# A two-layer AdaLN transformer kernel: the stage between its two attentions, rewritten

## The reference, cut to what matters

```
y = attn @ Wproj
y = jnp.transpose(y, (0, 2, 1)).reshape(Bx, Sx, Hx)
return y @ Wproj
```

## Time and profile before

| | us |
|---|---|
| median of 3 runs (lowest, highest) | 2282.1 (2281.39, 2282.92) |
| profiled execution, its own time | 2283.89 |
| profiled execution, span of the trace | 2282.1 |
| `layer0_attention` | 0 to 1798.9 of the span |
| `layer0_out` | 1798.95 to 1947.8 |
| the two functions of layer 1 | 1948.1 to 2282.1 |

### The profile page before, as it was taken

The page is one execution under the profiler, slowest core; times in us unless marked ns, Lnnn a source line. Parts: engine busy times, 40 slices in busy tenths (PEclk is TensorE's granted clock), DMA queues, the critical chain, the costliest instruction groups (busy, mean ns, idle before and its releaser), DMA issues. The chain is left out here.

```text
span 2282.1 us, 45663 instructions
## 1 busy us (share of the span) xinstructions
PE 2114.3 (93%) x16684; PEld 927.0 (41%) x16684; DVE 1758.6 (77%) x4030; ACT 1551.3 (68%) x3249; POOL 654.6 (29%) x1219
## 2 busy tenths in 40 slices
PE   6799999999999999999999999999999698989983
PEld 5143333333333333333333333333332287567731
DVE  3888888888888888888888888888885277244477
ACT  2078787877878787878787787878787445146633
POOL 2214142332313232414233231313211044000077
PEclk8599999999999999999999999999999799999955
DMA  5230312222121303031222212130200300000001
GB/s 150 41 63 11 67 25 52 38 39 50 27 50 32 65 12 71 10 67 24 54 38 40 50 27 50 32 64 8 45 2 2 103 0 0 1 1 2 1 28 46
DMA packets 129528, 84.74 MB, mean 37 GB/s; under 512 B 90273, under 2 KB 119073, under 8 KB 129313
## 3 DMA queue, kind: packets, MB, share of 16 engines
q1 hardware_dynamic: 129312, 81.91, 18.2%
HBM read 26.81 MB, written 16.78 MB: 19 GB/s over the span
## 5 line engine op out<-in xcount | busy, mean ns | idle before, releaser
L755 ACT ACTIVATE probs<-b_bank 128x512 f32<-128x512 f32 (+1 forms) x2304 | 1171.8, 578 | 347.2 <-PE b_bank L915 336.1
L632 DVE TENSOR_REDUCE m_part<-a_bank 128x1 f32<-128x512 f32 (+3 forms) x2048 | 1190.5, 634 | 153.1 <-PE a_bank L885 111.0
L915 PE MATMUL b_bank<-q_pack,k_pack 34*128 34x512 bf16 (+7 forms) x5120 | 920.8, 348 | 4.4 <-DMA q_pack<-m_rows 2.9
L885 PE MATMUL a_bank<-k_pack,q_pack 64*128 64x512 bf16 (+3 forms) x2560 | 811.1, 357 | 54.3 <-DVE m_part L632 30.7
L957 PE MATMUL acc<-probs,v_tile 128*32 128x512 f32 (+3 forms) x5120 | 586.7, 539 | 3.1 <-POOL probs L498 0.8
L915 PEld LDWEIGHTS b_bank<-q_pack,k_pack 34*128 34x128 bf16 (+1 forms) x5120 | 310.6, 94 | 511.9 <-ACT probs L755 436.3
L885 PEld LDWEIGHTS a_bank<-k_pack,q_pack 64*128 64x128 bf16 x2560 | 226.0, 94 | 343.7 <-DVE m_part L632 209.7
L498 POOL TENSOR_SCALAR_AFFINE_SELECT probs<-probs 128x512 f32<-128x512 f32 (+1 forms) x192 | 151.7, 790 | 609.7 <-ACT probs L755 609.6
L629 DVE CUSTOM_DVE_ANT_0 a_bank<-a_bank,mask_a 128x128 f32<-128x128 f32 (+3 forms) x512 | 241.8, 512 | 66.7 <-PE a_bank L885 66.7
L957 PEld LDWEIGHTS acc<-probs,v_tile 128*32 128x32 f32 x5120 | 107.8, 108 | 174.8 <-issue 117.8
L895 PE MATMUL a_bank<-future,pick 64*128 64x128 bf16 x1024 | 134.4, 219 | 0.0
(11 more groups left out here) (199 smaller groups left out, 1869.9 us busy)
## 6 DMA issues: line engine op xcount, KB each, us to landing
q_pack<-part SPq DMA_DIRECT2D x384, 64.0 KB, 2.3
k_pack<-part SPq DMA_DIRECT2D x192, 64.0 KB, 2.3
headT<-scratch SPq DMA_DIRECT2D x80, 128.0 KB, 4.0
scratch<-qkvT SPq DMA_DIRECT2D x16, 512.0 KB, 2.8
xg<-in_L_attn_x SPq DMA_DIRECT2D x16, 256.0 KB, 2.8
scratch<-qkvT SPq DMA_DIRECT2D x32, 128.0 KB, 2.7
q_pack<-m_rows SPq DMA_DIRECT2D x256, 2.0 KB
x<-in_L_attn_x SPq DMA_DIRECT2D x4, 1024.0 KB, 11.6
```

The costliest lines, as they stand in the source:

```text
L632: dve.tensor_reduce(out, bank[:, 0:w], AX.X, ALU.max).then_inc(a_maxed, 1)
L755: act.activation(probs[:, n % P_RING, h, at:C], b_bank[bank_no(("B", n, h))][:, at:C], ACT.Exp, scale=HD ** -0.5) \
L885: ins = pe.matmul(a_bank[at % A_RING][:, 0:w], q_pack[buf][rows, hp, 0, q:q + P], k_pack[buf][rows, 0, C * c:C * c + w], start=True, stop= ...
L915: ins = pe.matmul(b_bank[bank_no(slot)][:, at:at + C - q], k_pack[par][rows, n2, P * kt:P * (kt + 1)], q_pack[par][rows, h // 2, n2, C * j ...
```

## The change

Four things are changed, all in or for `layer0_out`.

1. The ten loads of weights are issued by SP in `layer0_attention`, at the start of its last group, into two tiles (`wqkv`, `qkvT`) that have had their last use by then. x is loaded in 32 transfers, four for each turn, and a turn's VectorE work waits for its own four (`x_in[n]`).
2. `attn` is laid out by row, [128, 2, 16, 256], so that TensorE can read a block of it as it lies. The product is associated the other way: TensorE makes `mid` = A_n^T wp_g (`middle`), ScalarE copies it, and TensorE makes wp^T mid. `stage`, the turn of A and the copy of it are gone.
3. The joint weights are made behind the first `middle`, and six of the gated rows are made by VectorE in turn 0.
4. The second norm is centred by ScalarE: GpSimd makes rs and a shift -mean*rs for both b at once (`scale_and_shift`, four instructions), and ScalarE centres block n-2 at the head of turn n, ahead of the copy of `mid`. All turns are written out, the hardware loop is gone.

```diff
+                if g == GROUPS - 1:
+                    sp.wait_ge(rows_ready, WPARTS * GROUPS)
+                    sp.wait_ge(rows_out, 48 * GROUPS)
+                    load_weights(sp)
                 if more:
                     load_x(g + 2, g + 2)
...
-                dst = attn[:, g, TB * j:TB * (j + 1), :].rearrange("p t (a e) -> p t a e", a=2)
+                dst = attn[:, g // KV, TB * j:TB * (j + 1), 2 * HD * (g % KV):2 * HD * (g % KV + 1)].rearrange("p t (a e) -> p t a e", a=2)
...
+            for n in range(NB):
+                for b in range(B):
+                    for k in range(2):
+                        sp.dma_start(x2[:, n, b, k, :], x[b, P * NB * k:P * NB * (k + 1), :].rearrange("(c n) d -> c n d", n=NB)[:, n, :]) \
+                            .then_inc(x_in[n], 16)
...
+            def scale_and_shift(n):
+                for b in range(B):
+                    pool.wait_ge(ln_step[1][b], 8 * n + 8)
+                wait_over(pool, xh_made[1][B - 1], n)
+                pool.tensor_tensor(ve[:, 1, :, :], mv[:, 1, :, :, 1], eps[:, :, :], ALU.add).then_inc(shift_step, 1)
+                pool.tensor_tensor(minus[:, :, :], zero[:, :, :], mv[:, 1, :, :, 0], ALU.subtract).then_inc(shift_step, 1)
+                pool.wait_ge(shift_step, 4 * n + 2)
+                pool.tensor_tensor(rs[:, 1, :, :], ve[:, 1, :, :], half[:, :, :], ALU.pow).then_inc(shift_step, 1)
+                pool.wait_ge(shift_step, 4 * n + 3)
+                pool.tensor_tensor(shift[:, :, :], minus[:, :, :], rs[:, 1, :, :], ALU.mult).then_inc(shift_step, 1)
 
             def turn(n, a, bb, c):
                 if a:
                     for b in range(B):
-                        deviation(n, 0, b)
+                        deviation(n, b)
                 if bb:
-                    for b in range(B):
-                        deviation(n - 1, 1, b)
+                    scale_and_shift(n - 1)
...
-                    for b in range(B):
-                        centre(m, 1, b, lambda k: x2[:, bass.ds(upto(m), 1), b, k, :].rearrange("p m d -> p (m d)"), h_turned)
...
         @block.scalar
             def turn(n, a, bb, c):
+                if c:
+                    m = n - 2
+                    act.wait_ge(shift_step, 4 * m + 4)
+                    for b in range(B):
+                        wait_over(act, h_turned, 2 * m + b - 1)
+                        for k in range(2):
+                            ins = act.activation(xh[:, 1, b, k, :], x2[:, m, b, k, :], ACT.Identity, bias=shift[:, b, k:k + 1],
+                                                 scale=rs[:, 1, b, k:k + 1])
+                        ins.then_inc(xh_made[1][b], 1)
                 if a:
                     for b in range(B):
...
+                        act.wait_ge(mid_made, 2 * n + b + 1)
+                        wait_over(act, z_made, 2 * n + b - 1)
+                        act.activation(mid[:, b, :, :].rearrange("p k d -> p (k d)"), bank[b][1][:, :], ACT.Copy).then_inc(mid_taken, 1)
...
         @block.tensor
+            def middle(n):
+                for b in range(B):
+                    wait_over(pe, x2_made, 2 * n + b - 3)
+                    for k in range(2):
+                        for t in range(2):
+                            ins = pe.matmul(bank[b][1][:, D * k:D * (k + 1)], attn[:, b, 2 * n + t, P * k:P * (k + 1)],
+                                            wp_g[:, b, t, :], start=t == 0, stop=t == 1)
+                    ins.then_inc(mid_made, 1)
 
             def turn(n, a, bb, c):
                 if a:
+                    if n == 0:
+                        pe.wait_ge(scaled, 2)
+                    middle(n)
+                if n == 0:
+                    joint_weights()
...
                 if a:
                     for b in range(B):
-                        pe.wait_ge(y_taken, upto(2 * n + b + 1))
+                        pe.wait_ge(mid_taken, 2 * n + b + 1)
+                        wait_over(pe, x1_made, 2 * n + b - 1)
                         for cc in range(2):
-                            for t in range(2):
-                                ins = pe.matmul(bank[b][0][:, D * cc:D * (cc + 1)], y[:, b, t, P * cc:P * (cc + 1)],
-                                                wp_g[:, b, t, :], start=t == 0, stop=t == 1)
+                            for k in range(2):
+                                ins = pe.matmul(bank[b][0][:, D * cc:D * (cc + 1)], wp[:, k, P * cc:P * (cc + 1)], mid[:, b, k, :],
+                                                start=k == 0, stop=k == 1)
                         ins.then_inc(z_made, 1)
```

More of the change, by code:

```diff
@@ L997, in _, with layer0_out @@
                     score_maxima(u)
[L999 removed]
+def layer0_out(nc, sems, keep, weights, w_loaded, x):
     ident, colmod, rowmod, attn, x2, h1T, w1T, woT, last_rows = keep
+    wp, wq_in, wo_in, f_in, rows_in, fv_in, fc_in = weights
     with ExitStack() as ctx:
@@ L1047, in layer0_out, with run @@
         ln_step = [[sem(f"ln_step{n}{b}") for b in range(B)] for n in range(2)]
-        ve_made = [[sem(f"ve_made{n}{b}") for b in range(B)] for n in range(2)]
-        rs_made = [[sem(f"rs_made{n}{b}") for b in range(B)] for n in range(2)]
+        ve_made = [sem(f"ve_made{b}") for b in range(B)]
+        rs_made, shift_step = [sem(f"rs_made{b}") for b in range(B)], sem("shift_step")
         xh_made = [[sem(f"xh_made{n}{b}") for b in range(B)] for n in range(2)]
         NB = S // ROWS
[L1052 to L1063, removed]
+        GATED = 6
+        def run(turn):
+            for n in range(NB + 2):
+                turn(n, n < NB, 1 <= n <= NB, n >= 2)
         def wait_over(eng, s, count):
@@ L1087, in _ @@
         @block.gpsimd
         def _(pool):
[L1089 to L1097, removed]
+            pool.memset(half[:, :, :], -0.5).then_inc(half_set, 1)
@@ L1112, in turn @@
                                            ALU.add).then_inc(x1b_made, 1)
-            run(pool, turn)
+            run(turn)
         @block.vector
@@ L1185, in _ @@
+            run(turn)
         @block.scalar
         def _(act):
-            def stage(n):
-                for b in range(B):
-                    for t in range(2):
-                        ins = act.activation(o_in[:, b, t, :].rearrange("p (g e) -> p g e", g=KV).unsqueeze(2),
-                                             attn[:, KV * b:KV * (b + 1), bass.ds(upto(2 * n + t), 1), :], ACT.Copy)
-                    ins.then_inc(o_copied, 1)
-            stage(0)
-            def turn(n, a, bb, c):
+            def turn(n, a, bb, c):
+                if c:
[7 more added lines that the diff above has]
+                        ins.then_inc(xh_made[1][b], 1)
@@ L1224, in turn @@
                         ins.then_inc(h_taken, 1)
-            run(act, turn)
+            run(turn)
         @block.tensor
@@ L1309, in turn @@
                         ins.then_inc(f_made, 1)
-            run(pe, turn)
+            run(turn)
 def layer1_attention(nc, sems, keep, aoT, v1):
```

166 lines of the change are left out of this document (74 added, 92 removed).

## The result

The changed kernel takes 2290.9 us (median of 9 runs, 2288.32 to 2293.05) and the kernel before 2283.4 (9 runs beside them, 2281.39 to 2286.07). The ratio is 1.0032, with an interval of 1.0022 to 1.0043: slower, by 7.5 us between the medians. The forecast was 2289, range 2277 to 2295, with slower as the likeliest case.

What follows compares the result with a forecast made beforehand. TensorE sets the pace before, VectorE close behind; afterwards a ring of waits through ScalarE's queue does. Terms -18.7 + 0 + 22.0 + 3.4 = +6.7 on the 2282.1 median give 2288.8, said as 2289, range 2277 to 2295.

Steps and rivals of the forecast that it cites:

- set-up, start to z(0): From the stage's start to its first product z: the 11.2 us wait for weights goes, -18.7 us (-21.7 to -14.0).
- z(0) to z(1): From turn 0's product z to turn 1's: nothing that counts changes, term 0, and 10.05 us stays.
- six turns: From z of turn 1 to z of turn 7: 102.6 us against 80.55, +22.0; +13.0 with a clock that holds.
- tail: From z of turn 7 to the end of the copies into h1T: 31.7 us against 28.3, +3.4.
- Layer 0: Ten weight issues at its last group, 4 to 7 us within 27.8 us of SP's waiting: no cost.
- the 1806 assumed: Set-up: timeline point near which TensorE's clock rises to full, so `middle` runs 10 of 16 instructions at half.
- The rival of a set-up at half for long: Set-up up to +4.7, part of a rival with a dearer pow: +10 to +15, 2292 to 2297, chance 0.13.
- The ring: In the turns, z waits for `mid`, queued behind ScalarE's older centring, which needs the previous z: 15.6 us a turn.
- The pow on four columns: GpSimd's pow for the shift, in the turns: 0.69 us taken, up to 1.2 possible, +0.5 a turn kept for the range.
- The clock's part: Clock falls in each 2.7 us TensorE gap; z's eight b = 0 instructions at half add 1.8: 17.4 a turn.
- clock holds: Rival: TensorE keeps full clock through the turns' 2.7 us gaps, -4.1 us in all, 2278; chance 0.23.
- The ring does not bind: Rival: TensorE's own work sets the turn at 12.2 us, -26 in all, 2256; chance 0.12.

Runs made afterwards that it cites:

- experiment 4: The changed kernel with the ten weight loads issued at the start of `layer0_out` again, ahead of the loads of x: 2301.62 us, ratio 1.0085 to the kernel before.
- experiment 1: The changed kernel with only ScalarE's order altered, the copy of `mid` ahead of the second centring in all turns: 2257.03 us, ratio 0.9898 to the kernel before.
- experiment 3: The changed kernel with the second centring back on VectorE, early loads and the other association kept: 2262.31 us, ratio 0.9911 to the kernel before.
- experiment 2: The changed kernel with six products of no use on TensorE ahead of z in turns 2 to 7: 2280.77 us, ratio 0.9992 to the kernel before.
- experiment 6: The kernel of experiment 5, with GpSimd's x1b waiting in turn 0 for VectorE's first centring: 2251.31 us, ratio 0.9852 to the kernel before.
- experiment 5: The kernel of experiment 1, with block 7's last product and its copy ahead of block 6's turn and centring in turn 8: 2258.17 us, ratio 0.9885.
- experiment 7: The kernel of experiment 5, with five products of no use on TensorE at the start of `layer1_out`: 2253.04 us, ratio 0.9870 to the kernel before.

## Why the prediction was right

The forecast was 6.7 us more (2288.8 - 2282.1); it is 7.0 between the spans and 7.5 between the medians. Point by point, each term against what it measured:

| term | forecast | measured | changed minus before |
|---|---|---|---|
| set-up, start to z(0) | -18.7 | -19.5 | 10.44 - 29.98 |
| z(0) to z(1) | 0 | +0.1 | 10.17 - 10.05 |
| six turns | +22.0 | +23.4 | 103.97 - 80.55 |
| tail | +3.4 | +3.2 | 31.47 - 28.31 |
| sum | +6.7 | +7.2 | span +7.0 |

The sum came nearer than its terms: the set-up brought 0.8 more than forecast and the turns cost 1.4 more, and these go against each other. That is luck of the size of 1 us; without it the forecast would still be in its range.

**Layer 0.** The ten issues cost nothing, as put; experiment 4 shows it from the other side.

**Set-up.** The mechanism was as described: TensorE starts at once, `middle` is next, no wait for a weight. The size was off by 0.8. The clock rose earlier than the 1806 assumed (it was 0.57 on average over 1802 to 1804 and 1.00 from 1804 on): `middle` ran 4.82 us from 1801.30 where 10 of 16 instructions at half would be 5.9. The rival of a set-up at half for long is out.

**The turns.** The ring is shown by experiments 1 and 3, which break it in two different ways and both find 12.8 to 13.0 a turn on average, and its length by experiment 2, and by the one turn of experiment 4 in which the clock held: 15.8 against 15.6. Two links were mis-sized. The pow on four columns took 1.01 us, between the 0.69 taken and the 1.2 kept as a bound; with the gaps the shift came 1.9 after the last aggregate, not 1.6. Against that, from the start of the centrings to that of `mid` was 1.98, not 2.2. The clock's part is 1.6 a turn (17.4 less 15.8) against 1.8, so that four turns came out at 17.37 to 17.42, forecast 17.4. The first of the six took 15.70. The second took 18.74: z(2) had the clock at half for nearly all its length (6.78 us). That turn alone is the 1.4 by which the term is off; why the clock stayed down longer there than later is not settled, and in experiment 4 it was z(6). The picture of where the half clock falls was too simple, too. The prediction had the eight instructions for b = 0 at half and charged 1.8 for them. In z(3) the clock fell only after 1.1 us: x1 of b = 0 came 0.8 late (2.81 after the start of z, 1.98 at full), and x1 of b = 1 another 0.8 behind it.

**The clock.** The rival "clock holds", given 0.23, is refuted for this kernel. TensorE was idle for 2.77 to 2.79 us ahead of each of z(2) to z(7), and all six ran in part at half (6.78 to 5.33 us in place of 3.62), and experiment 2 gives its price as 9 us for six turns, 10 in the times. The Trainium skill, "TensorE: Matmul & The Clock Gate", section "Why this matters for your kernels", warns of idle gaps of about 3 us and more, and by that rule these gaps would have passed. The measurement decides: they did not, and in experiment 6 a gap of 1.93 us did not either (`middle` at 5.41). That the clock had survived 3.00 us once was no reason to lean on the rule. The trace of the kernel before had a further gap of this size beside that one, and the four turns of a tile behind it took 1.11 us, not 0.66:

```profile
1934.55 1.11 PE L1297 MATMUL bank<-ident,xh 128*128 128x128 f32 x4 [2.54 <-DVE xh L1157]
```

The gap that the prediction reads as 2.1 us was 2.61 long in all, up to 1944.00. So that trace stood at two gaps of 2.5 to 2.6 us with a fall to one of 3.00 without. Nor is the fall certain: in experiment 4 the clock held through one gap of 2.79 and fell at five. The choice to let it fall at every gap came true in all six here; it was the likelier one, and not more than that.

**The ring does not bind** (0.12) is refuted for this kernel; its 12.2 a turn is 0.6 under what an order without the ring gives: 12.8 in experiment 1. The cause of the slowdown is thus neither the loads nor the association, which with the centring on VectorE bring some 20 us (ratio 0.9911), and not the centring on ScalarE as such (ratio 0.9898 behind `mid`), but one copy's place in one queue. Nor did that move bring anything at first, as the stages of experiments 1 and 3 show (127.5 and 125.7).

**The tail.** +3.2 against +3.4, with its order as put: z(7) at half, the centring ahead of f(7), and the turn and the first of f(7) at half after 5.40 us of standing still. The parts were less exact: f(7) started 17.8 us after z(7) and not 17.4, and from its start to the last aggregate it was 6.95, not 7.9, since the clock rose earlier in it (4.95 us, 5.93 before).

## What to carry to other kernels

When work is moved to an engine with time to spare, look at what is queued behind it: the busy share says nothing of an instruction that waits 6 us for its input with the critical copy behind it. Put the copy that the busiest engine waits for first in its queue, and the work on an older block after it. Where the busiest engine then waits, for 2.8 us as here, count the clock's fall as well: here a ring 3.0 us longer than TensorE's own pace (15.8 against 12.8) made turns that were 4.6 longer (17.4). And compare two variants by the stage that was edited as well as by the time: in experiments 1 and 3 the two rank them in opposite order.

## What the runs showed of the hardware

**Layer 1 had two lengths with the same instructions.** `layer1_out` took 117.7 to 118.1 us in the profiles of the kernel before, the changed kernel and experiments 3, 5 and 6, and 112.6 to 112.7 in those of experiments 1, 2 and 4. The attention of layer 1 goes with it, 214.1 to 214.5 us in experiments 1, 2 and 4 and 215.6 to 216.3 in the kernel before, the changed kernel and experiments 3, 5, 6 and 7; for that part no cause was looked for. In the last function the difference is the clock in its first microseconds. Experiment 1 by windows on TensorE, then the kernel before:

```profile
2143.00:2148.00 5.00, 5.00 (x17) 1.00 0.00 0
2148.00:2150.00 2.00, 2.00 (x6) 0.70 0.03 8
2150.00:2155.00 5.00, 5.00 (x10) 0.50 0.00 2
```

```profile
2165.30:2167.00 1.70, 1.70 (x5) 0.53 0.00 0
2167.00:2172.00 5.00, 5.00 (x9) 0.50 0.00 0
```

In one the function has 6 us at full before the clock falls, in the other it falls within a microsecond. Single runs of one kernel differ by as much: experiment 2 was profiled at 2274.7 with the short length, and its other runs lie at 2280 to 2284; experiment 6 was profiled at 2258.8 with the long one, and its others lie at 2249 to 2251.4. A difference of 5 to 7 us between two kernels here may be this alone; between experiments 1 and 5 it hid a gain of 5.6. In the profile of experiment 7, with its five products of no use, the function has nearly the short length; what decides it otherwise is not settled. The clock can also fall with no idle time ahead: in experiment 2, z(0) took 5.41 us, and TensorE had not stood still since the start of the stage, 9 us before; in the changed kernel the same instructions took 3.72.

**VectorE and GpSimd slow each other.** Two centrings took 2.62 us beside GpSimd's x1b and 0.73 without it. x1b took 2.54 for two beside those centrings, 2.48 beside an idle VectorE (turn 2 of the changed kernel), and 4.23 when it started among the six gated rows of experiment 6. So in the first meeting only VectorE paid, and in the second GpSimd. The Trainium skill, "GPSIMD Engine Reference", section "1. Specifications", says that the two engines share their way to SBUF and contend for some of VectorE's instructions; the runs agree, at 3.6 times the length for the centring. Moving one of the pair only moved the meeting.
